# A fused cross-attention and feed-forward kernel: dummy matmuls in TensorE's waits, first batches reordered, and the normalisation of q moved to GpSimd

## The reference

```python
x = x + gamma * xattn(layernorm(x), ctx, ctx)      # softmax(q.T k / 4) over 256 positions, per head
h = layernorm(x)
out0 = gelu(h @ W0a.T + b0a) @ W0b.T + b0b         # 256 -> 512 -> 256
out1 = relu(h @ W1a.T + b1a) @ W1b.T + b1b
x = x + where(argmax(h @ Wg.T) == 0, out0, out1)   # one of two experts per row
```

## Time and profile before

| | |
|---|---|
| median of 3 runs | 248.19 us (248.04 to 249.8) |
| profiled execution | 248.95 us |
| its span, first to last instruction | 247.1 us |
| busy: PE, DVE, ACT, POOL | 89%, 72%, 59%, 39% |
| HBM traffic over the span | 54 GB/s |

### The profile page before, as it was taken

The page is one execution under the profiler, slowest core; times in us unless marked ns, Lnnn a source line. Parts: engine busy times, 40 slices in busy tenths (PEclk is TensorE's granted clock), DMA queues, the critical chain, the costliest instruction groups (busy, mean ns, idle before and its releaser), DMA issues.

```text
span 247.1 us, 5173 instructions
## 1 busy us (share of the span) xinstructions
PE 219.7 (89%) x2001; PEld 171.3 (69%) x2001; DVE 178.1 (72%) x368; ACT 144.6 (59%) x217; POOL 96.3 (39%) x128
## 2 busy tenths in 40 slices
PE   0477988777898999999999999999999989979995
PEld 0344544444577888788878887888788877959995
DVE  7667476999875988698869886987597715445573
ACT  2012454856667758775877587758774786644140
POOL 8440231333984822482248224823361054032000
PEclk9999999886799999999999999999999999999999
DMA  4227777723330525161516250514111000000101
GB/s 170 100 71 246 247 298 224 273 90 129 88 131 36 183 66 175 10 233 64 176 25 216 65 175 21 178 49 150 20 49 53 16 24 3 21 21 3 41 5 42
DMA packets 18954, 25.86 MB, mean 105 GB/s; under 512 B 1946, under 2 KB 12530, under 8 KB 18674
## 3 DMA queue, kind: packets, MB, share of 16 engines
q1 hardware_dynamic: 17782, 22.63, 27.8%
q10 hardware_dynamic: 1148, 2.90, 3.3%
HBM read 11.28 MB, written 2.10 MB: 54 GB/s over the span
## 4 chain that ended last, share of the span: by engine, by line
PE 72%; DVE 12%; ACT 9%; issue 5%; POOL 0%; DVEq 0%; ACTq 0%; POOLq 0%
PE ff L822 18%; PE ff L852 11%; PE od L765 8%; PE st L753 8%; PE ff L863 6%; PE smax L741 5%; DVE nmax L396 4%; ACT P L600 4%; PE st L728 3%; PE od L773 3%; ACT hid L637 2%; PE od L780 2%; PE smax L714 2%; PE tr L795 1%; DVE qkst L184 1%
## 5 line engine op out<-in xcount | busy, mean ns | idle before, releaser
L600 ACT ACTIVATE P<-st 128x1024 f32<-128x1024 f32 x64 | 65.6, 1025 | 54.1 <-PE st L753 45.6
L396 DVE TENSOR_REDUCE nmax<-smax 128x4 f32<-128x1024 f32 x54 | 66.1, 1224 | 28.8 <-PE smax L741 28.2
L262 POOL TENSOR_TENSOR mv<-mv,power 128x1 f32<-128x1 f32 x31 | 18.3, 591 | 69.2 <-DVE mv L361 69.2
L280 POOL TENSOR_TENSOR hidL<-hid,hidH 128x1024 fp32r<-128x1024 f32 x13 | 31.0, 2387 | 20.6 <-DVE hidH L456 16.2
L822 PE MATMUL ff<-xnTh,w1h 128*128 128x256 f32 x128 | 37.5, 293 | 1.0 <-DVE y L494 1.0
L753 PE MATMUL st<-qkst 64*128 64x256 f32 x240 | 31.1, 338 | 6.6 <-ACT P L600 6.5
L637 ACT ACTIVATE hid<-ff,b1t 128x256 f32<-128x256 f32 x64 | 26.7, 470 | 17.4 <-PE ff L822 17.3
L822 PE MATMUL ff<-xnTh,w1l 128*128 128x256 f32 x128 | 36.0, 281 | 0.0
L822 PE MATMUL ff<-xnTl,w1h 128*128 128x256 f32 x128 | 35.9, 281 | 0.0
L765 PE MATMUL od<-P,vt 128*32 128x256 f32 x512 | 35.7, 426 | 0.1
L852 PE MATMUL ff<-w2h,hidH 128*128 128x256 f32 x124 | 34.2, 309 | 0.0
(11 more groups left out here) (100 smaller groups left out, 344.8 us busy)
## 6 DMA issues: line engine op xcount, KB each, us to landing
qkst<-parts SPq DMA_DIRECT2D x45, 256.0 KB
xv<-in_xv SPq DMA_DIRECT2D x16, 256.0 KB, 2.8
qk<-in_qk SPq DMA_DIRECT2D x15, 256.0 KB, 3.6
out<-y SPq DMA_DIRECT2D x16, 128.0 KB, 2.5
w1t<-in_w ACTq DMA_DIRECT2D x1, 1024.0 KB, 5.4
w2t<-in_w ACTq DMA_DIRECT2D x1, 1024.0 KB, 4.7
qk<-in_first SPq DMA_DIRECT2D x1, 256.0 KB, 3.8
qk<-in_first ACTq DMA_DIRECT2D x1, 256.0 KB, 3.9
```

The costliest lines, as they stand in the source:

```text
L262: pool.tensor_tensor(mv[:, b % 2, 11:12], mv[:, b % 2, 10:11], power[:, 0:1], ALU.pow).then_inc(s_rstd, 1)
L280: pool.tensor_tensor(hidL[:, units, :], hid[:, units, :], hidH[:, units, :], ALU.subtract).then_inc(s_hidL, 1)
L396: dve.tensor_reduce(nmax[:, c % 2, :, :, j].rearrange("p a e -> p e a"), (ff if c in WIDE and j % 2 else smax)[:, :, :, :], AX.X, ALU.max, ...
L600: act.activation(P[:, b % 2, j, :, :, :].rearrange("p e a l -> p (e a l)"), st[:, :, :, :].rearrange("p e a l -> p (e a l)"), ACT.Exp, sca ...
```

## The change

Four things are changed together.

1. Dummy matmuls. PE starts with 14 matmuls of 128x128 by 128x512 in bfloat16 (`spin`, into the still unused od), once DVE has written their operands. More of them stand in slots -6 to 15, as many as the table SPIN says (3 to 7 each, 65 in all besides the first 14). Those of slots up to 4 stand behind the slot's maxima; later ones stand behind waits that the next step needs anyway or nearly so (s_mrow, s_xTl, s_ods). Their results are overwritten.
2. First batches. The fill of stack 1 goes from DVE to ACT; ACT issues the loads of w1 and w2 (1 MB each) before slot -7 instead of in slots 2 and 6, and the four small loads in slot -2, not 0; batch 2's moments move from slot -7 to -4. w1h goes to slots 4 and 5, w1l and w2h to 8 and 9, w2l to 10 and 11, and `gate_and_bias` to slots 0 to 6.
3. From batch 2 on `q_norm` is POOL's, right behind `rstd`. Batch 1 keeps DVE's.
4. For both layernorms the addition of epsilon goes from DVE to POOL, with a wait between it and the power (batch 0 keeps its own).

```diff
-EARLY = {2: -7, 3: -2}
+EARLY = {2: -4, 3: -2}
+SPIN_FIRST = 14
+SPIN = {-6: 3, -5: 3, -4: 5, -2: 7, -1: 4, 0: 4, 1: 4, 2: 4, 3: 4, 4: 3, 6: 3, 7: 3, 8: 3, 10: 3, 11: 3, 12: 3, 14: 3, 15: 3}
...
-            def rstd(b, mv, count, s_var, s_rstd):
+            def rstd(b, mv, count, s_var, s_eps, s_rstd):
                 pool.wait_ge(s_var, count)
-                pool.tensor_tensor(mv[:, b % 2, 11:12], mv[:, b % 2, 10:11], power[:, 0:1], ALU.pow).then_inc(s_rstd, 1)
+                m = mv[:, b % 2, :]
+                pool.tensor_scalar_add(m[:, 10:11], m[:, 9:10], EPS).then_inc(s_eps, 1)
+                pool.wait_ge(s_eps, count)
+                pool.tensor_tensor(m[:, 11:12], m[:, 10:11], power[:, 0:1], ALU.pow).then_inc(s_rstd, 1)
+
+            def q_norm(c):
+                m, q = mv1[:, c % 2, :], qk[:, place(c, QK), 0, :]
+                pool.wait_ge(s_rstd1, c)
+                pool.tensor_scalar(q, q, m[:, 8:9], m[:, 11:12], ALU.subtract, ALU.mult).then_inc(s_qn, 1)
...
                     if c > 2:
-                        rstd(c, mv1, c, s_var1, s_rstd1)
+                        rstd(c, mv1, c, s_var1, s_eps1, s_rstd1)
+                        q_norm(c)
...
-                if b == 3 and j >= 2:
+                if b == 2 and j >= 2:
                     pool.wait_ge(s_w2h, j - 1)
...
-                if b == 3 and j < LC:
+                if b == 2 and j < LC:
                     pool.wait_ge(s_w1h, j + 1)
...
-            fill(dve, 1)
+            dve.memset(onesb[:, :], 1.0).then_inc(s_ones, 1)
+            dve.memset(hid[:, 0, :], 0.0).then_inc(s_ones, 1)
             fill(dve, 2)
...
-                for p in prepared(n - 1):
-                    q_norm(p)
-                if 6 <= n < 13:
-                    gate_and_bias(n - 6)
+                if 0 <= n < 7:
+                    gate_and_bias(n)
...
+            act.wait_ge(s_const, 1)
+            for side in range(2):
+
+                act.activation(qkst[:, 1, :, side, :], power[:, 0:1].unsqueeze(2).to_broadcast([128, PAIRS, L]), ACT.Copy,
+                               scale=-2.0 * side).then_inc(s_fill[1], 1)
+            act.dma_start(w1t[:, :, :, :].rearrange("p a e f -> p (a e f)"), w1).then_inc(s_w1, 16)
...
+            act.dma_start(w2t[:, :, :].rearrange("p u l -> p (u l)"), w2).then_inc(s_w2, 16)
...
+            def spin(bank, count):
+
+                for _ in range(count):
+                    pe.matmul(bank, onesb[:, :], hid[:, 0, :].bitcast(BF16), start=True, stop=True)
+
+            def spin_transposes(b):
+
+                if b >= 3:
+                    pe.wait_ge(s_xTl, b - 2)
+                spin(tr[:, :, :, :], SPIN.get(n, 0))
...
+            pe.wait_ge(s_ones, 2)
+            spin(od[:, :], SPIN_FIRST)
...
+                if n <= PAIRS:
+
+                    spin(od[:, :], SPIN.get(n, 0))
+                elif j == 0 and b < 4:
+                    pe.wait_ge(s_mrow, b)
+                    spin_transposes(b)
...
+                    if 1 <= b < 4:
+                        pe.wait_ge(s_mrow, b + 1)
+                        spin_transposes(b)
...
+                    if b < 4:
+                        pe.wait_ge(s_ods, b)
+                        spin(od[:, :], SPIN.get(n, 0))
```

More of the change, by code:

```diff
@@ L304, in _ @@
             pool.tensor_tensor(parts[:, 1, 3, :], qk[:, 0, 1, :], parts[:, 1, 2, :], ALU.subtract).then_inc(s_k1lo, 1)
-            rstd(1, mv1, 1, s_var1, s_rstd1)
+            rstd(1, mv1, 1, s_var1, s_eps1, s_rstd1)
             pool.wait_ge(s_hi, 1)
             pool.tensor_tensor(parts[:, 1, 0, :], qk[:, 0, 0, :], parts[:, 1, 1, :], ALU.subtract).then_inc(s_lo, 1)
-            rstd(2, mv1, 2, s_var1, s_rstd1)
-            pool.wait_ge(s_rstd1, 2)
+            rstd(2, mv1, 2, s_var1, s_eps1, s_rstd1)
+            q_norm(2)
+            pool.wait_ge(s_qn, 2)
             pool.wait_ge(s_lo, 1)
@@ L336, in _ @@
                 if j == 0 and b >= 2:
-                    rstd(b - 2, mv2, b - 1, s_var2, s_rstd2)
+                    rstd(b - 2, mv2, b - 1, s_var2, s_eps2, s_rstd2)
                 if j == 2 and b >= 2:
                     masks(b - 2)
-                if b == 3 and j >= 2:
+                if b == 2 and j >= 2:
                     pool.wait_ge(s_w2h, j - 1)
@@ L343, in _ @@
                     pool.tensor_tensor(w2l[:, half, :], w2t[:, half, :], w2h[:, half, :], ALU.subtract).then_inc(s_w2l, 1)
-                if b == 3 and j < LC:
+                if b == 2 and j < LC:
                     pool.wait_ge(s_w1h, j + 1)
                     pool.tensor_tensor(w1l[:, j, :, :], w1t[:, j, :, :], w1h[:, j, :, :], ALU.subtract).then_inc(s_w1l, 1)
-            rstd(B - 2, mv2, B - 1, s_var2, s_rstd2)
+            rstd(B - 2, mv2, B - 1, s_var2, s_eps2, s_rstd2)
             masks(B - 2)
             low_hidden(LAST - 1, 0)
-            rstd(B - 1, mv2, B, s_var2, s_rstd2)
+            rstd(B - 1, mv2, B, s_var2, s_eps2, s_rstd2)
             masks(B - 1)
@@ L354, in _, with moments @@
         def _(dve):
-            def moments(b, src, mv, count, s_stat, s_aggr, s_var):
+            def moments(b, src, mv, count, s_stat, s_var):
                 m = mv[:, b % 2, :]
@@ L358, in moments @@
                 dve.wait_ge(s_stat, count)
[L359 to L361 removed]
+                dve.bn_aggr(m[:, 8:10], m[:, 0:6]).then_inc(s_var, 1)
             def moments0():
@@ L379, in moments1, with q_norm1 @@
                 dve.wait_ge(s_qk[place(c, QK)], 16 * turn(c, QK))
[L380 to L384, removed]
+                moments(c, qk[:, place(c, QK), 0, :], mv1, c, s_stat1, s_var1)
+            def q_norm1():
+                m, q = mv1[:, 1, :], qk[:, place(1, QK), 0, :]
+                dve.wait_ge(s_rstd1, 1)
                 dve.tensor_scalar(q, q, m[:, 8:9], m[:, 11:12], ALU.subtract, ALU.mult).then_inc(s_qn, 1)
@@ L427, in moments2 @@
                 dve.wait_ge(s_x1, b + 1)
-                moments(b, x1[:, b % X1, :], mv2, b + 1, s_stat2, s_aggr2, s_var2)
+                moments(b, x1[:, b % X1, :], mv2, b + 1, s_stat2, s_var2)
             def x_norm(b):
@@ L527, in _ @@
             q_norm0(1)
-            q_norm(1)
+            q_norm1()
             for n in range(-LEAD, SLOTS):
@@ L680, in _ @@
                     high(p)
+                if n == -2:
+                    act.dma_start(wgb[:, :, :].rearrange("p a c -> p (a c)"), wg.partition_broadcast(128)).then_inc(s_small, 16)
+                    act.dma_start(gam[:, :], gamma.partition_broadcast(128)).then_inc(s_small, 16)
+                    act.dma_start(bias_f[:, :], b2.partition_broadcast(128)).then_inc(s_small, 16)
+                    act.dma_start(b1t[:, :], b1).then_inc(s_small, 16)
                 if k == 0 and 2 <= c <= B:
```

27 lines of the change are left out of this document (8 added, 19 removed).

## The result

| | before | after |
|---|---|---|
| median of 4 runs | 248.56 us (248.04 to 249.8) | 253.91 us (251.28 to 254.38) |
| profiled execution; span | 248.95; 247.1 | 253.63; 251.8 |
| first gemm1 matmul | 68.42 | 73.37 |
| from there to the end of the span | 178.7 | 178.4 |

The ratio is 1.018 with a 95% interval of 1.013 to 1.023: slower, by 1.3 to 2.3%. The executions of after lie 3.1 us apart (251.28 to 254.38), so its median is known to about 1 us only. The stage from the first gemm1 on kept its length, so the whole loss (5.0 us in the profiled executions) arose ahead of it, where the forecast had 6.7 us of gain.

What follows compares the result with a forecast made beforehand. It took PE's low clock until about 40.6 us, then DVE, to bound the part before slot 16. A 6.7 us gain there, with 0.2 lost at the end, made 248.95 into 242.3 profiled, 241.5 median; range 238.3 to 245.8.

Steps and rivals of the forecast that it cites:

- What bounds, and the rest: Ahead of slot 16: PE at 1.2 GHz until about 40.6 us, DVE from there to 57.6; 178.7 us after stay.
- Start: First dummies to batch 0's transposes: maxima0 at 7.75 instead of 8.10, transposes ending at 15.1 instead of 17.53; gain 2.4.
- Loads: w1 and w2 travelling at 5 to 15 us beside batch 1's stack copies: cost 0, bound 0 to 1.5 us.
- Rival (d): Early loads delay the first stack copies: +1.5, 243 us; chance 0.65 together with the main forecast.
- The new operation: q_norm on POOL, not in the trace: put at 0.55 us, between 0.40 and 0.72; adding epsilon 0.22.
- high(4) sooner: Slot 4: ACT's high(4) no longer waits for DVE's q_norm(4), so the exponential starts earlier; gain up to 0.9 us.
- Rounds: Float32 scores rounds before the first values: 2.4 us each instead of 3.2.
- Gain 4.5: After the rounds, transposes of batch 1's maxima end at 25.1 instead of 29.58; 3.9 left after dummies of slots 2 and 3.
- POOL's pile: POOL's row of work in slots 8 to 12: 14.3 us from 41.7, DVE waiting about 2 us before x_norm(1).
- Rival (c): POOL's pile costs nothing: 2 to 2.5 better, 239 to 239.5 us; chance 0.12 for this or better.
- (a): Clock not kept everywhere, with dents in slots 13 and 14 or the rounds: 243.5 to 246 us; chance 0.14.
- (b): Dummies don't lift the clock, or it falls before slot -1 and stays low: 254 to 257 us; chance 0.09.

Runs made afterwards that it cites:

- x9: The kernel before with only the dummies of slots 6 to 15; 248.66 us, ratio 1.000.
- x3: The changed kernel without any dummy matmul, all else as changed; 250.86 us, ratio 1.010 to before.
- x13: The kernel before with only the two 1 MB loads (w1, w2) in the change's early places; 250.14 us, ratio 1.005.
- x16: The changed kernel without dummies and with the weight splits in their old slots, early loads kept; 247.71 us, ratio 0.994 to before.
- x6: The changed kernel without dummies and with loads and weight splits in their old places; 245.39 us, ratio 0.988 to before.
- x1: The changed kernel with the four weight splits back in their old slots, loads and dummies as changed; 247.76 us, ratio 0.994 to before.
- x4: The kernel before with all the dummies alone, nothing else of the change; 249.54 us, ratio 0.998.
- x15: The changed kernel with only the first 14 dummies and those of slots -6 to 4; 252.53 us, ratio 1.005 to before.
- x2: The changed kernel with weight splits and the w1 and w2 loads back in their old places, all dummies kept; 244.98 us, ratio 0.985 to before.
- x18: The kernel before with q_norm on POOL from batch 2 on, nothing else; 246.83 us, ratio 0.991.
- x17: x6 with both additions of epsilon back on DVE; 245.57 us, ratio 0.986 to before.
- x7: x2 with q_norm back on DVE, epsilon additions still on POOL; 247.06 us, ratio 0.985 to before.

## Why the prediction was wrong, step by step

**What bounds, and the rest.** The low clock up to 40 us under a column of 1.00 was right (x9's and x3's first `values` takes 3.54 and 3.08 as well), and the stage behind the first gemm1 kept its length. The premise that the slow clock "is paid for" was read from the chain up to 30 us. From 40 us on the recorded dents cost little, as the prediction's own reading of DVE's 6.09 of 7.00 us should have said: x9 removes them for about 0.6 us.

**Start.** "`maxima0` starts at 7.75" was wrong by 1.95, and with it the step **Loads**, "I cost it at 0, bound 0 to 1.5". The prediction had the loads travel at 5 to 15 us; ACT issued w1 at 1.54, in front of the landing of q of batch 1, which batch 0's path waits for since DVE's order has the moments of batch 1 first. Measured cost 1.3 (x13) and 2.3 (x16 against x6), inside the bound and over it. PE stood 3.51 us, and the clock fell behind that, so the first `transpose_max` ended at 20.4 and not 15.1. In the four traces in which PE idled 2.46 to 3.91 us ahead of `maxima0` (x1, x4, after, x15) the products of the third pair ran at the low clock (2.08); in x2, with 0.99, they took 1.13. But the step was too large there too: from the start of `maxima0` to the end of the transposes it is 9.43 us in before, was forecast at 7.35 and is 8.16 in x2, a gain of 1.3 instead of 2.1. And the scores came 2.34 us behind the transposes "as before" in the forecast; it was 2.84 in after and 3.17 in x4, where seven dummies (slot -2) stand in front of them and end just when the scores begin. Rival (d) named the early loads but at a later place, the stack copies; both places are seen.

**The new operation.** A POOL q_norm was taken at 0.55 between 0.40 and 0.72. It is 1.25. The upper bound was too low: neither a copy nor a two-input subtract prices an operation with two per-partition scalars. What the Trainium skill says of one-input work ("GPSIMD Engine Reference", section "Engine selection": roughly line rate) holds for POOL's copy of 0.40, but not for this. On the chip the move still gained, 2.0 alone and 3.0 in the new order, more than the 0.9 that "high(4) sooner" had; part of the more is luck of the clock (x18). Epsilon was right at 0.22, and worth nothing (x17).

**Rounds.** 2.47 against a forecast of 2.4: right. That the gain then survives ("Gain 4.5") was wrong: the transposes of batch 1's maxima were forecast to end at 25.1, and ended at 33.18 in after, 30.06 in x4 and 29.04 in x2, against 29.58 in before. "If stack copies of batch 1 or 2 hold `maxima`" stands among the signs of failure, and that is what came: 1.71 us in after, 1.43 in x2, 2.67 for the row of maxima in x4, with the DMA engines at 0.94. The prediction had q_norm(2) move to 16.65 and priced it for ACT only, not for the copy behind it, and gave the faster rounds no price on the DMAs. Behind each of these waits the clock fell, and the dummies of slots 2 and 3 took 1.89 and 1.26 in after instead of 0.88 each, in front of the next products. `values(0)` came at 42.19 and not at 32.3, the largest single miss.

**POOL's pile.** 14.3 forecast; from 51.86 to the end of the power at 67.22 it was 15.4, the difference being mainly q_norm's 0.7. DVE's wait was forecast at 2 and was 3.23. "x_norm(0) next to w1l costs nothing": it took 1.54 and was indeed covered by DVE's later wait. The pile was placed 10 us too early (41.7 against 51.86). x_norm(1) was forecast 6.4 us earlier than in before (56.0 against 62.37) and came 4.9 later (67.26). The price of moving the pile, which no term of the sum named by itself, was 3.2 without dummies and 6.1 with them. Rival (c), that it costs nothing, is refuted.

**The sums.** Three slips are small beside this. The terms listed for the start add up to 14.7, not 15.1, mostly because the transposes themselves are not among them. From x_norm(1) to the first gemm1, 5.06 + 1.3 - 0.9 - 0.7 is 4.8, not 5.1 to 5.4. And 248.95 - 6.7 + 0.2 is 242.45, not 242.3.

**The rivals.** (a) had the dents but put them at 243.5 to 246 on top of a gain that wasn't there. (b) came nearest to the time, 254 to 257, for a reason that the trace contradicts in part: the dummies did lift the clock. They lifted it where PE then waited for DMAs and DVE, and it fell again where PE had to wait, and the low clock held for some 17 of the 52 us from 8 to 60 (mean clock 0.84, so 0.32 of the time at 0.5), a third and not the half from which (b) was to decide. What made up the time was the rest: the late DMAs, the early loads and the pile. The 0.09 on the slower side was far too little for a change whose four parts had each an unpriced effect on the others. The failed step is therefore not one number but the assumption under the sum: that a gain of PE in the rounds arrives at slot 16, with loads and pile at no cost on the way. What the runs put in its place: dummies -0.4 to +0.6 us with loads and splits in their old places (x2, x4), early loads +1.3 to +2.8, early splits +3.2 to +6.1, and the only gain, -3.5, from the new order together with POOL's q_norm.

## What to carry to other kernels

Dummy matmuls for the clock pay only where TensorE's own speed is what ends last: first look at the windows for the engine that is full beside PE, and at the DMA share, since faster PE rounds run into both. A load or a weight preparation moved "to a quiet time" must be followed through each order it now stands ahead of: here 1 MB issued at 1.5 us held a 256 KB load, and 9.4 us of POOL work moved one batch forward tied the whole start to batch 0. A small transfer that PE needs (8 KB, the row of the maxima) came 0.7 us or more later in each of the three runs in which a 256 KB load was issued just ahead of it. Change such things one at a time: here q_norm off DVE gained 2 to 3 us, loads and splits lost 5.5 between them, and the dummies, worth nothing by themselves, cost 2 to 3 on top once the splits were early.

## What was not expected of the hardware

- ACT's queue issued a DMA at 1.54 while the two activations that stand ahead of it in its stream ran from 2.73 to 4.73: the order on ACT's stream doesn't hold a DMA back behind them. "Strictly in the order of their own stream", as the description of the kernel has it, is true of ACT's activations and not of its DMA issues against them.
- POOL's subtract-and-multiply of 128x256 with two per-partition scalars takes 1.25 us, DVE's 0.41, POOL's copy 0.40.
- DVE's x_norm took 1.54 beside POOL's w1l, more than the 0.99 of before; it ended at 55.22, just behind w1l's end at 55.07. The Trainium skill's "SBUF — State Buffer", section "Who interferes with whom", has the two excluding each other for the instruction; the rows agree, and the earlier DVE meets the w1l, the longer it takes.
- The granted clock column stands at 1.00 from the start until its first fall, although the durations there are those of the low clock: in x3 `values(0)` takes 3.08 and in x9 3.54 where a full-clock one takes 1.93.

Open remain: whether the wait for the stack copy of batch 2 in after and x2 goes when its moments go back to slot -7; how the 2 to 3 us of q_norm divide into DVE's relief and luck of the clock; and what sets the clock's falls in the runs of x4, x7 and x15, whose times spread over 5.6 to 7.5 us.
